# State space layer on one core: where a scan gets its first state, and which engine adds seven of 48 sum units

## What is computed

```python
xz = xs @ in_proj_w.T
xin, z = split(xz, 2)
xin = silu(causal_conv4(xin) + conv_b)
dt, Bm, Cm = split(xin @ x_proj_w.T, [24, 40])
dt = softplus(dt @ dt_proj_w.T + dt_proj_b)
A = -exp(A_log)                               # 768 channels x 16 states
def step(h_prev, (x_t, dt_t, B_t, C_t)):
    h_new = exp(dt_t[..., None] * A) * h_prev + dt_t[..., None] * B_t * x_t[..., None]
    return h_new, einsum('bds,bs->bd', h_new, C_t)
y = (ys + xin * D) * silu(z)
out = layernorm(y @ out_proj_w.T) * ln_gamma + ln_beta
```

## Time and profile before

| | us |
|---|---|
| median of 3 runs (lowest, highest) | 5764.54 (5763.57, 5771.34) |
| the profiled execution, its own time | 5764.76 |
| its span in the trace | 5763.0 |
| first scan of the state space layer begins | 128.97 |
| last work of that layer on VectorE | 3468.7 |
| TensorE's mean granted clock, share of full speed | 0.954 |

### The profile page before, as it was taken

The page is one execution under the profiler, slowest core; times in us unless marked ns, Lnnn a source line. Parts: engine busy times, 40 slices in busy tenths (PEclk is TensorE's granted clock), DMA queues, the critical chain, the costliest instruction groups (busy, mean ns, idle before and its releaser), DMA issues. The chain is left out here.

```text
span 5763.0 us, 81471 instructions
## 1 busy us (share of the span) xinstructions
PE 5022.4 (87%) x30948; PEld 4080.8 (71%) x30948; DVE 4308.4 (75%) x4771; ACT 2958.0 (51%) x5242; POOL 2869.7 (50%) x3500
## 2 busy tenths in 40 slices
PE   4898999998989989999899877778878879999999
PEld 2776777776777767777777753565656669999998
DVE  1999999999999999999999986484847553333333
ACT  3766677766677766666666633131313223333332
POOL 3776777776776776777777634362535310000000
PEclk8999999999999999999999987788888889999999
DMA  2000000000000010000000011002020010010100
GB/s 72 1 16 27 9 9 9 9 23 20 9 9 9 16 31 13 9 9 9 9 9 9 5 40 60 20 25 74 25 74 13 28 54 25 25 34 25 34 25 21
DMA packets 88530, 136.93 MB, mean 24 GB/s; under 512 B 5284, under 2 KB 85184, under 8 KB 88140
## 3 DMA queue, kind: packets, MB, share of 16 engines
q1 hardware_dynamic: 88140, 131.72, 7.0%
HBM read 89.23 MB, written 42.47 MB: 23 GB/s over the span
## 5 line engine op out<-in xcount | busy, mean ns | idle before, releaser
L730 DVE TENSOR_TENSOR_SCAN a_h<-a_dA,pw 128x770 f32<-128x770 f32 x1152 | 2012.5, 1747 | 130.0 <-PE pw L448 128.8
L595 ACT ACTIVATE a_dA<-a_dt,a_Aneg 128x384 f32<-128x384 f32 x2304 | 1314.5, 607 | 185.6 <-DVE a_h L730 176.4
L869 POOL TENSOR_SCALAR a_dBT<-a_dtxT,a_BC 128x768 f32<-128x768 f32 x1152 | 1024.6, 906 | 448.6 <-PE pw L448 345.6
L458 PEld LDWEIGHTS pw<-g_ident,a_h 128*128 128x128 f32 x6912 | 796.2, 142 | 491.8 <-DVE a_acc L750 197.6
L458 PE MATMUL pw<-g_ident,a_h 128*128 128x128 f32 x6912 | 968.4, 277 | 157.7 <-DVE a_acc L750 121.6
L750 DVE SCALAR_TENSOR_TENSOR a_acc<-pw,a_BC,a_acc 128x768 f32<-128x768 f32 x960 | 960.7, 1001 | 84.3 <-PE pw L458 56.7
L447 PE MATMUL pw<-g_ident,a_dBT 128*128 128x128 f32 x6912 | 948.1, 274 | 4.8 <-POOL a_dBT L869 4.8
L447 PEld LDWEIGHTS pw<-g_ident,a_dBT 128*128 128x128 f32 x6912 | 795.5, 141 | 6.5 <-POOL a_dBT L869 5.4
L1829 DVE TENSOR_TENSOR d_hf<-d_hf,ps 128x384 f32<-128x384 f32 x288 | 159.0, 554 | 560.7 <-ACT d_hf L1759 553.5
L821 POOL TENSOR_TENSOR a_xin<-a_xin,a_tm 128x384 f32<-128x384 f32 x432 | 432.9, 1002 | 32.7 <-ACT a_tm L517 7.7
L406 PE MATMUL ps<-a_xn,a_WinT 128*128 128x384 f32 x864 | 365.6, 525 | 30.7 <-ACT a_sz L573 15.1
(11 more groups left out here) (243 smaller groups left out, 9666.0 us busy)
## 6 DMA issues: line engine op xcount, KB each, us to landing
b_xs<-x SPq DMA_DIRECT2D x36, 576.0 KB, 5.0
a_xs<-in_x SPq DMA_DIRECT2D x24, 576.0 KB, 3.9
x<-a_xs SPq DMA_DIRECT2D x24, 576.0 KB, 3.0
b_x<-x SPq DMA_DIRECT2D x24, 576.0 KB, 4.4
e_xs<-x SPq DMA_DIRECT2D x24, 576.0 KB, 3.9
out<-e_xs SPq DMA_DIRECT2D x24, 576.0 KB, 3.0
a_sx<-in_x SPq DMA_DIRECT2D x54, 192.0 KB, 2.4
x<-b_x SPq DMA_DIRECT2D x16, 576.0 KB, 3.1
```

What stands on the lines that cost most here:

```text
L458: t = e.transpose(m["pw2"][:, c * 128:(c + 1) * 128], m[f"a_h{g % 2}"][:, c, 1 + tb * 128:1 + (tb + 1) * 128], ident[:])
L595: e.activation(m[f"a_dA{idx // 2 % NDA}"][:, idx % 2, 1:T + 1], m[f"a_dt{k % 2}"][:, c, :], ACT.Exp, scale=m["a_Aneg"][:, c, n:n + 1]).the ...
L730: e.tensor_tensor_scan(m[f"a_h{g % 2}"][:, c:c + 2, :].rearrange("p c t -> p (c t)"), m[f"a_dA{pi % NDA}"][:].rearrange("p c t -> p (c t)" ...
L869: t = e.tensor_scalar(m[f"a_dBT{g % 2}"][:, tb, :], m[f"a_dtxT{o}"][:, tb, :], m[f"a_BC{o}"][:, tb, n:n + 1], 1.0, ALU.mult, ALU.mult)
```

## The change

The matmul that put the first states into `pw` is gone. The columns that the scan needs between the channel blocks are now constants in `pw` (0, and between the two blocks 1 and 0), written once by VectorE at the start, and a pair has 2 x 384 + 3 = 771 columns. The first states go into the decays instead: after every second decay ScalarE copies two columns from `a_st` (or `a_zero`) into columns 0 and 386 of the `a_dA` buffer. The scan begins with 1, so that decay times 1 plus 0 is the first state; column 385 has decay 0 and input 1, which sets the running value back to 1. `inputs` now ends with the sixth transpose, which increments `pe_b`. `a_exp` counts three instructions a pair instead of two. `LENT` has seven units instead of five.

```diff
-COL = 511 - (T + 1)
+PAIR = 2 * T + 3
+COL = 511 - (T + 2)
-        m.new(f"a_dA{i}", [128, 2, T + 1])
+        m.new(f"a_dA{i}", [128, PAIR])
-        m.new(f"a_h{i}", [128, 6, T + 1])
+        m.new(f"a_h{i}", [128, 3, PAIR])
-LENT = (20, 22, 24, 38, 41)
+LENT = (20, 22, 24, 26, 38, 41, 43)
+def first_col(c):
+    return 1 + c % 2 * (T + 2)
 def inputs(k, p):
-        w.wait_ge("p_const", 4)
-        if q > 0:
-            w.wait_ge("p_st", g - NS + 1)
-        first = m["a_st"][:, c:c + 2, p // 3] if q > 0 else m["a_zero"][:]
+        w.wait_ge("v_w", 5)
         for h in range(2):
             for tb in range(TB):
-                at = COL + h * (T + 1) + 1 + tb * 128
-                e.transpose(ps[:, at:at + 128], ...)
-        e.matmul(ps[:, COL:COL + T + 2:T + 1], ident[:], first, start=True, stop=True, skip_group_check=True).then_inc(s["pe_b"], 1)
+                at = COL + 1 + h * (T + 2) + tb * 128
+                t = e.transpose(ps[:, at:at + 128], ...)
+        t.then_inc(s["pe_b"], 1)
 def exp(idx):
             w.wait_ge("v_scan", idx // 2 - NDA + 1)
-            e.activation(m[f"a_dA{idx // 2 % NDA}"][:, idx % 2, 1:T + 1], ..., ACT.Exp, ...).then_inc(s["a_exp"], 1)
+            dA = m[f"a_dA{idx // 2 % NDA}"]
+            e.activation(dA[:, first_col(c):first_col(c) + T], ..., ACT.Exp, ...).then_inc(s["a_exp"], 1)
+            if c % 2:
+                if k % NQ > 0:
+                    w.wait_ge("p_st", g - NS + 1)
+                w.wait_ge("p_const", 4)
+                e.activation(dA[:, 0:T + 3:T + 2], m["a_st"][:, c - 1:c + 1, n] if k % NQ > 0 else m["a_zero"][:], ACT.Copy).then_inc(s["a_exp"], 1)
 def l0_dve(e, m, w):
+    for i in range(2):
+        e.memset(m[f"pw{i}"][:, COL:COL + T + 3:T + 2], 0.0).then_inc(s["v_w"], 1)
+        e.memset(m[f"pw{i}"][:, COL + T + 1:COL + T + 2], 1.0).then_inc(s["v_w"], 1)
 def scan(k, p):
-        w.wait_ge("a_exp", 2 * pi + 2)
+        w.wait_ge("a_exp", 3 * pi + 3)
+        w.wait_ge("v_w", 5)
-        e.tensor_tensor_scan(..., m[f"pw{pi % 2}"][:, COL:COL + 2 * (T + 1)], 0.0, ALU.mult, ALU.add).then_inc(s["v_scan"], 1)
+        e.tensor_tensor_scan(m[f"a_h{g % 2}"][:, p % 3, :], m[f"a_dA{pi % NDA}"][:], m[f"pw{pi % 2}"][:, COL:COL + PAIR], 1.0, ALU.mult, ALU.add).then_inc(s["v_scan"], 1)
 def l0_pool(e, m, w):
-        e.memset(m[f"a_dA{i}"][:, :, 0:1], 0.0).then_inc(s["p_const"], 1)
+        e.memset(m[f"a_dA{i}"][:, T + 1:T + 2], 0.0).then_inc(s["p_const"], 1)
 def kept(g):
         w.wait_ge("v_scan", 3 * (g + 1))
-        w.wait_ge("pe_b", 3 * g + 3)
-        e.tensor_copy(m["a_st"][:, :, g % NS], m[f"a_h{g % 2}"][:, :, T]).then_inc(s["p_st"], 1)
+        w.wait_ge("a_exp", 9 * (g + 1))
+        e.tensor_copy(m["a_st"][:, :, g % NS].rearrange("p (a b) -> p a b", b=2), m[f"a_h{g % 2}"][:, :, T:PAIR:T + 2]).then_inc(s["p_st"], 1)
```

More of the change, by code:

```diff
@@ L385, in pre_pe @@
         w.wait_ge("v_dt3", k + 1)
-        w.wait_ge("v_w", 3)
+        w.wait_ge("v_w", 7)
         e.matmul(ps[:, 0:T], m["a_Wdt3"][:, i * 128:(i + 1) * 128], m["a_dt3"][:], start=True, stop=True).then_inc(s["pe_V"], 1)
@@ L433, in inputs @@
     def inputs(k, p):
-        pi, q = PAIRS * k + p, k % NQ
+        pi = PAIRS * k + p
         g, c = NS * k + p // 3, 2 * (p % 3)
@@ L439, in inputs @@
         w.wait_ge("v_scan", pi - 1)
-        w.wait_ge("p_const", 4)
-        if q > 0:
-            w.wait_ge("p_st", g - NS + 1)
-        first = m["a_st"][:, c:c + 2, p // 3] if q > 0 else m["a_zero"][:]
+        w.wait_ge("v_w", 5)
         for h in range(2):
             for tb in range(TB):
-                at = COL + h * (T + 1) + 1 + tb * 128
-                e.transpose(ps[:, at:at + 128], m[f"a_dBT{g % 2}"][:, tb, (c + h) * 128:(c + h + 1) * 128], ident[:])
-        e.matmul(ps[:, COL:COL + T + 2:T + 1], ident[:], first, start=True, stop=True, skip_group_check=True).then_inc(s["pe_b"], 1)
+                at = COL + 1 + h * (T + 2) + tb * 128
+                t = e.transpose(ps[:, at:at + 128], m[f"a_dBT{g % 2}"][:, tb, (c + h) * 128:(c + h + 1) * 128], ident[:])
+        t.then_inc(s["pe_b"], 1)
     def turned(hh):
@@ L457, in turned @@
         for c in range(6):
-            t = e.transpose(m["pw2"][:, c * 128:(c + 1) * 128], m[f"a_h{g % 2}"][:, c, 1 + tb * 128:1 + (tb + 1) * 128], ident[:])
+            t = e.transpose(m["pw2"][:, c * 128:(c + 1) * 128], m[f"a_h{g % 2}"][:, c // 2, first_col(c) + tb * 128:first_col(c) + (tb + 1) * 128], ident[:])
         t.then_inc(s["pe_h"], 1)
@@ L542, in pre_act @@
         w.wait_ge("p_dtx", 6 * (k - 1))
-        w.wait_ge("a_exp", STEPS * (k - 1))
+        w.wait_ge("a_exp", 3 * PAIRS * (k - 1))
         e.activation(dt[:, i, :], ps[:, 0:T], ACT.Abs, bias=pv[:, i, 5:6])
@@ L594, in exp @@
             w.wait_ge("v_scan", idx // 2 - NDA + 1)
-            e.activation(m[f"a_dA{idx // 2 % NDA}"][:, idx % 2, 1:T + 1], m[f"a_dt{k % 2}"][:, c, :], ACT.Exp, scale=m["a_Aneg"][:, c, n:n + 1]).then_inc(s["a_exp"], 1)
+            dA = m[f"a_dA{idx // 2 % NDA}"]
+            e.activation(dA[:, first_col(c):first_col(c) + T], m[f"a_dt{k % 2}"][:, c, :], ACT.Exp, scale=m["a_Aneg"][:, c, n:n + 1]).then_inc(s["a_exp"], 1)
+            if c % 2:
[3 more added lines that the diff above has]
+                e.activation(dA[:, 0:T + 3:T + 2], m["a_st"][:, c - 1:c + 1, n] if k % NQ > 0 else m["a_zero"][:], ACT.Copy).then_inc(s["a_exp"], 1)
     def weighed(k, u):
@@ L719, in l0_dve @@
     e.tensor_copy(m["a_Wdt3"][:], m["a_acc0"][:, 0, :]).then_inc(s["v_w"], 1)
-    w.wait_ge("v_w", 2)
+    w.wait_ge("v_w", 6)
     e.tensor_tensor(m["a_Wdt3"][96:128, :], m["a_acc0"][96:128, 0, :], m["a_Wdt3"][96:128, :].bitcast(F32), ALU.subtract).then_inc(s["v_w"], 1)
@@ L724, in scan @@
     def scan(k, p):
-        pi, g, c = PAIRS * k + p, NS * k + p // 3, 2 * (p % 3)
+        pi, g = PAIRS * k + p, NS * k + p // 3
         w.wait_ge("pe_b", pi + 1)
-        w.wait_ge("a_exp", 2 * pi + 2)
+        w.wait_ge("a_exp", 3 * pi + 3)
+        w.wait_ge("v_w", 5)
         w.wait_ge("pe_h", 3 * (g - 1))
         w.wait_ge("p_st", g - 1)
-        e.tensor_tensor_scan(m[f"a_h{g % 2}"][:, c:c + 2, :].rearrange("p c t -> p (c t)"), m[f"a_dA{pi % NDA}"][:].rearrange("p c t -> p (c t)"),
-                             m[f"pw{pi % 2}"][:, COL:COL + 2 * (T + 1)], 0.0, ALU.mult, ALU.add).then_inc(s["v_scan"], 1)
+        e.tensor_tensor_scan(m[f"a_h{g % 2}"][:, p % 3, :], m[f"a_dA{pi % NDA}"][:], m[f"pw{pi % 2}"][:, COL:COL + PAIR], 1.0, ALU.mult, ALU.add).then_inc(s["v_scan"], 1)
     def weighed(hh):
@@ L1598, in l12_sp @@
     w.wait_ge("v_st", GN * NB)
-    w.wait_ge("a_exp", STEPS * (NCH - 1))
+    w.wait_ge("a_exp", 3 * PAIRS * (NCH - 1))
     w.wait_ge("p_dbt", NS * (NCH - 1))
```

## The result

The changed kernel takes 5680.32 us in the median of 4 runs (5679.07 to 5683.06), against 5767.94 for the kernel before on the same chip. The ratio is 0.9847 with a 95% interval of [0.983, 0.9864], so it is faster by 1.5%. The prediction said 5670 us in a range of 5590 to 5735.

A forecast was written before the change was run, and what follows sets the result against it. VectorE was taken as the bound, TensorE close behind; the terms summed to 4.15 us a chunk, 91 us over 22 chunks plus 4 for first and last, so 5764.8 - 95 = 5670 us, range 5590 to 5735.

The forecast's parts named there:

- (a): Pairs 9 to 17 of a chunk: pitch of 2.83 us falls to 2.61, gain 1.5 us (1.2 to 2.0).
- (b): Pair 23, where ScalarE reads the output product late: three to four copies add 0.45 us, net loss 0.2 a chunk.
- (c): Pairs 25 to 27: two or three removed matmuls in the chain, gain 0.6 us a chunk (0.3 to 1.3).
- (d): Pairs 31 and 32: lent unit 26's read lengthens the chain of six dt products, loss 0.25 us a chunk.
- (e): Pair 37: a chain starting at a VectorE instruction holds two of the matmuls, gain 0.45 us a chunk (0.2 to 0.7).
- (f): Pairs 39 to 44: six pairs with the matmul in a TensorE, ScalarE, TensorE chain, gain 1.4 us (0.9 to 2.0).
- (g): Pair 3: gain 0.2 us a chunk (0 to 0.2).
- (h): Lent unit 43 at pair 46, where TensorE has little side work: 0.55 of 0.91 us kept a chunk (0.3 to 0.75).
- (i): Every scan grows by one column: loss 0.1 us a chunk.
- The clock rival: Stretches of transposes alone run TensorE at 1.2 GHz; with ten such pairs a chunk, slower at 5953 us; chance 0.03.
- More comes back: VectorE runs at its floor except at pair 23: 7.5 us a chunk expected, 9.7 at most, 5590 us; chance 0.20.
- ScalarE's rival: Copies costing over 0.43 us, or late decays, make ScalarE the limit; at 0.47 us a copy, 5781 us; chance 0.05.

The follow-up runs named there:

- the early read: The changed kernel with ScalarE reading the third output product ahead of the norm and decays that stood before it: 5633.9 us, ratio 0.9776.

## Why the prediction was right, and where it was off

Per usual chunk, gains in us (minus is a loss). A place is measured with the pairs beside it that the change moved, so some run over more pairs than in the prediction:

| place | predicted | measured |
|---|---|---|
| (a) pairs 9 to 17 | 1.5 | 1.56 |
| (b) pair 23 | -0.2 | -1.04 |
| (c) pairs 24 to 27 | 0.6 | 0.25 |
| (d) pairs 28 to 32, with unit 26 | -0.25 | -0.02 |
| (e) pair 37 | 0.45 | 0.41 |
| (f) pairs 38 to 44 | 1.4 | 1.48 |
| (g) pair 3 | 0.2 | 0.20 |
| (h) pairs 45 to 47, unit 43 | 0.55 | 0.84 |
| (i) longer scan | -0.1 | -0.04 in the 17 pairs outside the places |
| sum | 4.15 | 3.66 |

The time came out 10 us over the forecast, and 3.66 us a chunk for 4.15 hides larger misses that partly cancel: (b) and (c) together are 1.2 us too high, (d) and (h) together 0.5 too low. The longer scan is 0.002 us a pair, 0.1 us over 48 pairs as predicted; in the places it lies inside the other gains.

**What bounds the kernel** held: TensorE's 0.22 us counted only where VectorE waited for TensorE, and the run with the matmul kept shows that it is the source of the gain. Of 10.6 us a chunk that TensorE was relieved of, under half came back.

**Place (b)** is the step that failed. As far as it went it was right: four copies, at 0.09 instead of my 0.13, delayed ScalarE's read, and without the clock the pair takes 4.09 us instead of 4.19, so 0.1 gained rather than 0.2 lost. What I left out is what the delay does to TensorE's clock. I priced the copies as time on the path, and not as a longer pause of TensorE. The pause grew from 1.53 to 2.00 us, nearly 0.4 of it by the copies and 0.1 because the faster TensorE reaches the same wait earlier, and behind it the clock fell in fifteen chunks, 1.1 us a usual chunk in the mean. Without the copies the clock stayed up and a chunk took 1.9 us less: that is the whole price of the copies, of which their own time is 0.4. In four chunks (1, 3, 10 and 16) it stayed up with them, and these gained 5.1 to 5.2 us each. I had looked for a falling clock among the transposes, at the end of the chunk, and not at a growing pause. **Place (c)** was mis-sized for the same reason: with the pause filled it gives 0.55, about the predicted 0.6.

**The clock rival** had the right effect by the wrong cause, so one of the prediction's signs of being wrong, a granted clock below 1.00 in the middle of the layer, did appear. After the last L412 of the chunk TensorE does nothing but 36 transposes until 1058.64; the windows row there:

```profile
1053.00:1059.00 6.00, 4.67 (x38) 4.06 (x38) 6.00 (x5) 6.00 (x15) 5.63 (x8) 1.00 0.02 4
```

The clock stays at 1.00, so the rule that the prediction cites, that a transpose does not count for the clock as a matmul does (the Trainium skill, "TensorE: Matmul & The Clock Gate", Part 4: PE-mode transpose), did not bring a loss here.

**Unit 26** (d) was read rightly: it costs more than it saves, 0.70 us net by the runs with and without it. **More comes back** did not happen either. With the early read the changed kernel gains 6.2 us a chunk (130.2), between my 4.15 and this rival's 7.5. **ScalarE's rival** did not come: a copy's step is 0.09 us and the tipping point was 0.43. **Unit 43** (h) was sized too low by 0.3: pair 46 takes 1.71 us from scan to scan, hardly more than the 1.66 after which an undisturbed scan is followed.

Of the other signs, the chunk near 132 us, the pitch of 2.60 in pairs 10 to 13 and the unchanged pairs 29 to 32 (12.05 us, from 12.03) came; the copies' step was shorter; pair 23's wait is 1.50 us with the clock up and 2.2 to 3.2 with it down, neither within 1.6 to 2.1; and the waits for TensorE were not halved. They hold the falls of the clock, some 1.1 us a chunk, and 2.4 of the 3.5 us that a chunk lost are VectorE's own work, not waits.

## What to carry to other kernels

Time taken off an engine that is not the bound comes back only in the pairs where the bound waits for it; find those in the timeline of one period and add them up, rather than taking a share of busy time. When an engine gets more work, ask not only whether its delay lies on the path, but also whose pause the delay makes longer, and whether that is TensorE with its clock. Here the copies, four of them at 0.09 us ahead of one read, cost 1.9 us a chunk, and moving one read forward was worth more (2.5 us a chunk) than two lent units. Work handed to another engine is worth its time only where the next scan is ready: unit 43 gave 0.84 us, unit 26 cost 0.70, unit 33 gave nothing. So try each place by itself.

## What the runs showed of the hardware

A pause of TensorE of 2.00 us between matmuls was followed by some 3 us at the low level of its clock in fifteen of nineteen chunks of the changed kernel, in thirteen of them with five lent units and in seven without unit 26. A pause of 1.90 us was in four of nineteen, and pauses of 1.63 and 1.53 us never were. Filling the pause with useless products made the kernel 0.4% faster. A ScalarE copy of two columns takes 0.19 us but holds the engine for only 0.09 us. And two kernels whose layer took the same 3136 us differed by 14 us in total, with TensorE's clock lower in one of them in layers that neither had changed, so below 0.3% a total alone does not judge an edit here.
